# A Mamba-2 scan in the second layer of a two-layer kernel: squares summed ahead of the product with ones, and B held twice per chunk

## The chip, the core and the metric

The kernel runs on one core of a Trainium2 chip. Five engines run their own instruction streams and meet at semaphores: TensorE (PE; its weight loads are listed as PEld), VectorE (DVE), ScalarE (ACT), GpSimd (POOL) and SyncE (SP), which mostly issues DMAs. The metric is the device time in microseconds of one execution.

## What is computed

Four sequences of 512 tokens with 256 features pass through two layers. Each layer adds to the tokens the output of a state-space scan and that of a mixture of experts (a shared expert and 16 routed ones). The change lies in the scan of the second layer, a Mamba-2 block with 64 heads of 8 columns and a state of 128:

```python
proj = hidden_states @ in_proj_w.T
gate = proj[..., :D_IN]                       # D_IN = 512
xBC = proj[..., D_IN:D_IN + CONV_DIM]         # x (512), B (128), C (128)
...
conv = conv_b + sum((conv_w[:, i] * xp[:, i:i + l, :] for i in range(K)))   # K = 4
xBC = jax.nn.silu(conv)
...
Y_diag = jnp.einsum('bcthn,bcshn,bhcts,bcshp->bcthp', Ch, Bh, Lmat, x)
states = jnp.einsum('bcshn,bhcs,bcshp->bchpn', Bh, decay_states, x)
...
Y_off = jnp.einsum('bcthn,bchpn,bhct->bcthp', Ch, prev, jnp.exp(dA_cum))
...
y = y + D[None, None, :, None] * x
hg = y * jax.nn.silu(gate)
var = jnp.mean(hg * hg, axis=-1, keepdims=True)
y = hg * jax.lax.rsqrt(var + EPS) * norm_w
return y @ out_proj_w.T
```

## The kernel before

The second layer's scan (`scan1_tensor`, `scan1_scalar`, `scan1_vector`, `scan1_sync`) goes through the four sequences (b) one after the other. Features lie on the partitions, in groups of 128: four groups (G1 = 4) of x and of the gate, one of B (`xB`), one of C (`xC`). All of it is fp32 but for the decay matrices.

**Projections.** For each sequence ten products of 128x512 (NPROJ = 10; L1819). The first six are B, C and the four groups of x: ScalarE copies one out of its bank into `xpad` (L1914) and `cv` (L1915), VectorE adds three taps of the convolution (L2035), ScalarE takes tanh (L1888), VectorE finishes silu (`silu_of`, L1978) into `xB`, `xC` or `xb`. The silu of projection n-1 stands ahead of the convolution of projection n on VectorE. The last four are the gate (L1926, L2046). LATE = 3: the last output tile of the sequence before is made behind the fourth projection (n = 3).

**Chunk steps.** The 512 tokens are cut into 8 chunks (CH) of 64 (Q). In step s TensorE first makes bank `gb`: the products of B and C (L1831) in columns 0:64 and B transposed (L1833) in columns 64:192, both written twice, to partitions 0:64 and 64:128, since the two halves of the heads lie there; then x transposed (L1840), the new state of the chunk before (L1846), for each of four groups the exponents (L1809, L1811), the products with the masked matrix (L1860) of the chunk before, and at the end of the step the product of C with the state S (L1877, 64 rows wide). VectorE multiplies x with its weights (L2071), forms the masked matrices (`products`, L1985), and carries S on (L2083, L2088). Every second step closes a tile of 128 tokens: y is added up (L2059, L1869), `gated` (L1993) and `gate` (L2001) make `hg`, ScalarE squares it into `sq` (128 x 4 groups x 128 tokens, L1893), and from step 4 on `output` makes the out-projection of a tile (L1796, four products of 256 columns) and the sum of its squares over all 512 features: four products of `sq` with two columns of ones (L1798), accumulated. ScalarE copies both into `ob` (L1898). Tile 3 of a sequence is made among the next one's projections, and that of the last sequence at the very end, where `mean_square` and `add_scan1` follow.

**Order.** Everything is written by hand; a "tick" counter spreads the routed experts' work (three ticks for a tile of 128 rows, 48 tiles) over projections and groups: `expert_tensor` (L1374, L1380, L1386, L1393), `expert_scalar` (L1402 to L1417), `expert_vector` (L1425 and L1427, which makes `hid`, for which TensorE waits at L1380). It ends with the tenth projection of the last sequence. Banks 0 and 1 are a ring (`PIECES`, `make`, `take`, `taken`) for projections, `gb`, exponents and outputs. SyncE loads the decay rows `crow` of a chunk when S of the chunk before is ready (L1743), and the experts' weights (L1437, L1438).

## Time and profile before

| | us |
|---|---|
| median of 3 runs | 1323.91 (1321.68 to 1327.96) |
| profiled execution | 1332.39, its span 1330.7 |
| PE / DVE / ACT / POOL busy | 1078.8 / 897.7 / 492.1 / 451.5 |
| mean granted clock of TensorE | 0.898 |

The profile is of one execution; its durations hold for that one. The second layer's scan begins at 781 us and fills the rest of the span. A row of the timeline has the start, the duration, engine and line, what is written and read, and in brackets how long the engine had been idle and who released it. A matmul's duration reaches to the end of its passage through the array, so that neighbours overlap: what a product costs is the distance between starts. The chain of work that ended last has the same columns, but there the durations are those stretches that follow one another without overlap. An fp32 product leaves two records (xN counts records).

### The profile page before, as it was taken

The page shows a single profiled execution, that of the slowest core. Times are in us where ns is not written, and L with a number is a line of the kernel's source. Part 1 is how long each engine was busy: PE and PEld are TensorE (multiplying, and loading weights), DVE is VectorE, ACT ScalarE, POOL GpSimd, SP SyncE. Part 2 cuts the span into 40 slices and gives each one's busy share as a digit, 9 for nine tenths or more (in the row PEclk, how much of TensorE's full clock was granted, in tenths as well). Part 3 has the DMA queues.
Part 4 walks back from the last instruction along what each step waited for, and adds up shares of the span by engine and source line. Part 5 has one row for each costly group of instructions (what it writes and reads, how often), then busy time and mean ns, then how long its engine had stood idle before and what let it go on. Part 6 is the DMA issues. An engine that isn't in the chain of part 4 may idle for free.

```text
span 1330.7 us, 19215 instructions
## 1 busy us (share of the span) xinstructions
PE 1078.8 (81%) x6464; PEld 643.8 (48%) x6464; DVE 897.7 (67%) x1480; ACT 492.1 (37%) x1110; POOL 451.5 (34%) x334
## 2 busy tenths in 40 slices
PE   2989895877878778874767758999799979998795
PEld 2545453444444444443634434565455645555354
DVE  3287576789998889897355646565566565565685
ACT  2111032445544445541220134344444454344432
POOL 1000000588888888761100152233132323231000
PEclk9799898799998889986787888899899979899898
DMA  9900071488888878889520123444254424442111
GB/s 373 311 4 0 7 189 63 76 153 153 149 151 144 149 135 150 153 133 228 99 64 1 24 81 87 101 97 99 55 132 87 110 60 103 91 96 55 25 54 63
DMA packets 116997, 143.30 MB, mean 108 GB/s; under 512 B 35830, under 2 KB 103142, under 8 KB 116710
## 3 DMA queue, kind: packets, MB, share of 16 engines
q0 software_dynamic: 34464, 77.92, 32.4%
q1 hardware_dynamic: 82438, 64.14, 17.4%
q8 instruction: 55, 0.90, 0.3%
q14 instruction: 40, 0.33, 0.1%
HBM read 72.80 MB, written 39.46 MB: 84 GB/s over the span
## 4 chain that ended last, share of the span: by engine, by line
PE 49%; DVE 24%; DMA 9%; issue 6%; ACT 5%; POOL 4%; SPq 3%; ACTq 0%; DVEq 0%; POOLq 0%
PE bank L666 6%; PE bank L1386 4%; PE bank L678 4%; PE bank L1819 4%; PE bank L1393 4%; PE bank L979 3%; PE bank L1860 3%; DVE xnT L1112 3%; DMA sum<-yo,to_i 3%; DVE areaB L1112 2%; DVE cv L2035 2%; PE bank L1796 2%; PE bank L1809 2%; PE bank L1811 2%; DMA wr<-in_gate 2%
## 5 line engine op out<-in xcount | busy, mean ns | idle before, releaser
L1459 POOL DMA_INDIRECT sum<-yo,to_i x48 | 76.5, 1593 | 327.6 <-ACT yo L1413 317.5
L1139 POOL DMA_INDIRECT xg<-xn_d,token_i x80 | 97.3, 1217 | 252.6 <-DVE to_i L441 157.9
L1132 POOL DMA_INDIRECT sum<-yo,to_i x80 | 157.9, 1974 | 44.8 <-issue 33.4
L979 PE MATMUL bank<-areaA,xgT 128*128 x320 | 131.7, 540 | 26.2 <-ACT xgT L1036 16.7
L996 PE MATMUL bank<-areaA,hidT 88*128 x320 | 95.7, 424 | 41.6 <-ACT hidT L1046 32.8
L1985 DVE TENSOR_TENSOR areaD<-areaD,gb 128x512 f32<-128x512 f32 x128 | 87.7, 689 | 35.6 <-ACT areaD L1947 24.7
L1112 DVE TENSOR_TENSOR_SCAN xnT<-areaB,xnT 128x1024 f32<-128x1024 f32 x44 | 100.9, 2292 | 3.5
L1947 ACT ACTIVATE areaD<-bank 128x512 f32<-128x512 f32 x128 | 76.1, 596 | 66.5 <-PE bank L1811 61.5
L979 PEld LDWEIGHTS bank<-areaA,xgT 128*128 128x128 f32 x320 | 61.9, 213 | 72.6 <-issue 57.7
L1819 PE MATMUL bank<-xnT,w_in 128*128 128x512 f32 x160 | 88.1, 681 | 10.0 <-POOLq L1482 10.0
L996 PEld LDWEIGHTS bank<-areaA,hidT 88*128 88x128 f32 x320 | 57.7, 200 | 76.2 <-issue 71.1
L666 PE MATMUL bank<-xnT,areaB 128*128 128x512 f32 x192 | 88.4, 608 | 0.8 <-DVE y L696 0.8
L1028 ACT ACTIVATE areaB<-delta,a_neg 128x1022 f32<-128x1022 f32 x64 | 72.8, 1138 | 24.2 <-DVE y L1092 17.9
L2035 DVE SCALAR_TENSOR_TENSOR cv<-xpad,conv_w,cv 128x512 f32<-128x512 f32 x72 | 54.0, 750 | 25.8 <-ACT cv L1915 24.1
L1393 PE MATMUL bank<-wst,xgT 128*128 128x352 f32 x192 | 67.7, 476 | 0.0
L687 ACT ACTIVATE areaB<-bank 128x512 f32<-128x512 f32 x24 | 14.3, 597 | 135.9 <-PE bank L666 135.9
L1386 PE MATMUL bank<-wst,hidT 88*128 88x256 f32 x192 | 61.0, 446 | 1.8 <-ACT hidT L1407 1.2
L1860 PEld LDWEIGHTS bank<-areaD,xq 128*32 128x32 f32 x2048 | 35.1, 111 | 55.2 <-issue 43.0
L1041 ACT ACTIVATE act_t<-bank 128x176 f32<-128x176 f32 x80 | 25.2, 315 | 95.9 <-PE bank L979 91.6
L949 PE MATMUL bank<-parts,pick 96*128 96x512 bf16 x128 | 41.3, 406 | 23.0 <-DVE areaB L1116 10.7
L666 PEld LDWEIGHTS bank<-xnT,areaB 128*128 128x128 f32 x192 | 36.1, 194 | 48.5 <-issue 45.3
L678 PE MATMUL bank<-areaB,y 128*128 128x256 f32 x192 | 48.6, 414 | 13.3 <-DVE x L708 11.2
(329 smaller groups left out, 2271.7 us busy)
## 6 DMA issues: line engine op xcount, KB each, us to landing
y<-xnT POOLq DMA_DIRECT2D x22, 1024.0 KB
wst<-gu_f SPq DMA_DIRECT2D x96, 176.0 KB
y<-areaB POOLq DMA_DIRECT2D x10, 1024.0 KB
wst<-down_f SPq DMA_DIRECT2D x48, 176.0 KB
gu_f<-in_gu POOLq DMA_DIRECT2D x1, 5632.0 KB, 19.0
areaA<-in_gu SPq DMA_DIRECT2D x2, 2816.0 KB
sum<-yo SPq DMA_DIRECT2D x2, 2176.0 KB, 17.9
down_f<-in_down POOLq DMA_DIRECT2D x1, 2816.0 KB, 24.8
```

The source lines that it names most:

```text
L666: last = nc.tensor.matmul(bank[:, b, :], w[:, k, f * P:(f + 1) * P], xnT[:, k, c * 512:(c + 1) * 512], start=(k == 0), stop=(k == KD - 1))
L678: last = nc.tensor.matmul(bank[:, 4 + n % 2, 0:D], shT[:, (c * F + f) % shT.shape[1], j * P:(j + 1) * P], sd[:, f, :], start=(f == 0), sto ...
L979: last = nc.tensor.matmul(bank[:, GB + q % 2, 0:2 * FI], xgT[:, q % 2, k, :], wgu0_of(e, k), start=(k == 0), stop=(k == KD - 1))
L996: last = nc.tensor.matmul(bank[:, HY, 0:D], hidT[:, q % 2, h, :], wd0_of(e, h), start=(h == 0), stop=(h == 1))
L1112: nc.vector.tensor_tensor_scan(h, dA[:, u % 2, :], h, 0.0, ALU.mult, ALU.add).then_inc(da_free, 1)
L1132: nc.gpsimd.indirect_dma_start(sum0_d[q % 2], bass.IndirectOffsetOnAxis(ap=to_i[:, q:q + 1], axis=0), yo[:, q % 5, :], None, compute_op=AL ...
L1139: nc.gpsimd.indirect_dma_start(xg[:, q % 5, :], None, xn_d[0], bass.IndirectOffsetOnAxis(ap=token_i[:, q:q + 1], axis=0)).then_inc(s.gathe ...
L1386: last = nc.tensor.matmul(bank[:, eb, 0:D], hidT[:, (q - 1) % 2, h, :], wd_of(q - 1, h), start=(h == 0), stop=(h == 1))
L1393: last = nc.tensor.matmul(bank[:, eb, 0:2 * FI], xgT[:, q % 2, k, :], wgu_of(q, k), start=(k == 0), stop=(k == KD - 1))
L1819: last = nc.tensor.matmul(o, w_in[:, k, col:col + P], xnT[:, k, b * L:(b + 1) * L], start=(k == 0), stop=(k == KD - 1))
L1985: nc.vector.tensor_tensor(mm[:, g, :].rearrange("p (j t) -> p j t", t=Q), ex[:, g % 2, :].rearrange("p (j t) -> p j t", t=Q), gb[:, step % ...
L2035: last = nc.vector.scalar_tensor_tensor(cv[:, n % 2, :], xpad[:, n % 2, i:i + L], conv_w[:, j, i:i + 1], cv[:, n % 2, :], ALU.mult, ALU.add)
```

## The change

`sum_squares` on VectorE adds the four groups of `sq` into `sq_sum` (128x128) with one reduce, and TensorE waits for it (`sq_summed`) ahead of the whole output; one product with ones remains. `xB` now holds each chunk's 64 columns twice, written by two silu instructions, and each product for `gb` has all 128 columns as its weight and writes both halves at once. The reduces for tiles 0 to 2 stand at the third group of steps 4, 6 and 8, behind `products` and ahead of the addition to S, those for tile 3 behind the third projection's convolution of the next sequence, and the last one behind the last `gate`.

```diff
--- before.py
+++ after.py
@@ -1260,9 +1260,10 @@
         cv = sb("cv", [P, 2, L], F32, c1)
         tb = sb("tb", [P, 2, L], F32, c1)
         xb = sb("xb", [P, G1, L], F32, c1)
-        xB = sb("xB", [P, L], F32, c1)
+        xB = sb("xB", [P, CH, 2, Q], F32, c1)
         xC = sb("xC", [P, L], F32, c1)
         sq = sb("sq", [P, G1, P], F32, c1)
+        sq_sum = sb("sq_sum", [P, P], F32, c1)
         ob = sb("ob", [P, PAIRS, D + 2], F32, c1)
         dw = sb("dw", [P, 2, CH, NB, HP], F32, c1)
         ecn = sb("ecn", [P, PAIRS, NB, HP, 2], F32, c1)
@@ -1293,6 +1294,7 @@
             sem(n) for n in ("xt_full", "xt_used", "st_full", "s_ready", "yo_full", "m_ready", "m_used"))
         y_tok, yt_full, y_read, hg_ready, sq_ready, ssq_in, ssq_out, x_done = (
             sem(n) for n in ("y_tok", "yt_full", "y_read", "hg_ready", "sq_ready", "ssq_in", "ssq_out", "x_done"))
+        sq_summed = sem("sq_summed")
         crow_in = [sem(f"crow_in{k}") for k in range(2)]
         cpc_in = [sem(f"cpc_in{k}") for k in range(2)]
         dec_in = [sem(f"dec_in{k}") for k in range(2)]
@@ -1791,12 +1793,10 @@
             def output(b, t):
 
                 o, full = make(pe, b, "out", t)
-                pe.wait_ge(sq_ready, b * PAIRS + t + 1)
+                pe.wait_ge(sq_summed, b * PAIRS + t + 1)
                 for g in range(G1):
                     nc.tensor.matmul(o[:, 0:D], hg[:, g, t * P:(t + 1) * P], w_out[:, g, :], start=(g == 0), stop=(g == G1 - 1))
-                for g in range(G1):
-                    last = nc.tensor.matmul(o[:, D:D + 2], sq[:, g, :], ones[:, 0:2], start=(g == 0), stop=(g == G1 - 1))
-                last.then_inc(full, 1)
+                nc.tensor.matmul(o[:, D:D + 2], sq_sum[:, :], ones[:, 0:2], start=True, stop=True).then_inc(full, 1)
 
             def segment(b, step, g):
 
@@ -1827,11 +1827,9 @@
                     at = slice(step * Q, (step + 1) * Q)
                     if step < CH:
                         o, full = make(pe, b, "gb", step)
-                        for r in (0, Q):
-                            nc.tensor.matmul(o[r:r + Q, 0:Q], xB[:, at], xC[:, at], start=True, stop=True)
-                        for r in (0, Q):
-                            last = nc.tensor.matmul(o[r:r + Q, Q:Q + P], xB[:, at], ident[:, :], start=True, stop=True)
-                        last.then_inc(full, 1)
+                        both_b = xB[:, step, :, :].rearrange("p r t -> p (r t)")
+                        nc.tensor.matmul(o[:, 0:Q], both_b, xC[:, at], start=True, stop=True)
+                        nc.tensor.matmul(o[:, Q:Q + P], both_b, ident[:, :], start=True, stop=True).then_inc(full, 1)
 
                         if b * CH + step:
                             pe.wait_ge(xt_used, b * CH + step)
@@ -1974,8 +1972,14 @@
             def silu_of(b, n):
                 v.wait_ge(conv_tanh, b * 6 + n + 1)
                 j = CONV_ORDER[n]
-                to = (xb[:, j, :] if j < G1 else (xB, xC)[j - G1][:, :])
-                nc.vector.scalar_tensor_tensor(to, tb[:, n % 2, :], 1.0, cv[:, n % 2, :], ALU.add, ALU.mult).then_inc(conv_out, 1)
+                if j == G1:
+                    by_chunk = [z[:, n % 2, :].rearrange("p (k t) -> p k t", t=Q) for z in (tb, cv)]
+                    for r in range(2):
+                        last = nc.vector.scalar_tensor_tensor(xB[:, :, r, :], by_chunk[0], 1.0, by_chunk[1], ALU.add, ALU.mult)
+                else:
+                    to = xb[:, j, :] if j < G1 else xC[:, :]
+                    last = nc.vector.scalar_tensor_tensor(to, tb[:, n % 2, :], 1.0, cv[:, n % 2, :], ALU.add, ALU.mult)
+                last.then_inc(conv_out, 1)
 
             def products(b, step, g):
 
@@ -1999,6 +2003,14 @@
                 at = slice(t * P, (t + 1) * P)
                 v.wait_ge(y_read, b * PAIRS + t + 1)
                 nc.vector.scalar_tensor_tensor(hg[:, :, at], hg[:, :, at], 0.5, gz[:, :, at], ALU.mult, ALU.mult).then_inc(hg_ready, 1)
+
+            def sum_squares(b, t):
+
+                v.wait_ge(sq_ready, b * PAIRS + t + 1)
+                if b or t:
+                    n = b * PAIRS + t - 1
+                    taken(v, n // PAIRS, "out", n % PAIRS)
+                nc.vector.tensor_reduce(sq_sum[:, :], sq[:, :, :].rearrange("p g t -> p t g"), X, ALU.add).then_inc(sq_summed, 1)
 
             def mean_square(b):
 
@@ -2044,6 +2056,8 @@
                         o, free = take(v, b, "proj", n)
                         v.wait_ge(gate_th, b * G1 + g + 1)
                         nc.vector.scalar_tensor_tensor(gz[:, g, :], tb[:, g % 2, :], 1.0, o, ALU.add, ALU.mult).then_inc(free, 1)
+                    if b and n == LATE - 1:
+                        sum_squares(b - 1, PAIRS - 1)
                     if b and n == LATE + 1:
                         mean_square(b - 1)
                     if b and n == LATE + 3:
@@ -2076,6 +2090,8 @@
                         expert_vector(v, step_tick(b, step, g))
                         if step < CH:
                             products(b, step, g)
+                        if g == 2 and step % 2 == 0 and step > 2:
+                            sum_squares(b, (step - 4) // 2)
                         if g == 1 and 1 < step < CH:
                             v.wait_ge(yo_full, b * (CH - 1) + old)
                             state_of(v, b, old)
@@ -2096,6 +2112,7 @@
                         add_experts(SUMS.index(step))
                 gated(b, PAIRS - 1)
                 gate(b, PAIRS - 1)
+            sum_squares(NB - 1, PAIRS - 1)
             mean_square(NB - 1)
             add_scan1(NB - 1)
             add_experts(NB - 1)
```

The lines of the changed kernel have other numbers: L1798 is then the out-projection (before L1796), L1799 the product with ones (L1798), L1832 B transposed (L1833), L1838 x transposed (L1840), L1844 the state (L1846), L1875 C with S (L1877), L1867 y added up (L1869), L1989 `products` (L1985), L2104 the addition to S (L2088), L2013 the reduce.

TensorE at the turn from step 4 to 5 of the first sequence, before: `ys` added up, the output, C with S, then the chunk's own products.

```order
L1869 MATMUL bank<-ident,ys 128x128 x4
L1796 MATMUL bank<-w_out,areaD 128x256 x4
L1798 MATMUL bank<-ones,sq 128x2 x4
L1877 MATMUL bank<-S,xC 64x512
L1831 MATMUL bank<-xC,xB 64x64 x2
L1833 MATMUL bank<-ident,xB 64x128 x2
L1840 MATMUL bank<-ident,xb 64x64 x8
L1846 MATMUL bank<-xd,gb 128x512
```

The same place in the changed kernel:

```order
L1867 MATMUL bank<-ident,ys 128x128 x4
L1798 MATMUL bank<-w_out,areaD 128x256 x4
L1799 MATMUL bank<-ones,sq_sum 128x2
L1875 MATMUL bank<-S,xC 64x512
L1831 MATMUL bank<-xC,xB 128x64
L1832 MATMUL bank<-ident,xB 128x128
L1838 MATMUL bank<-ident,xb 64x64 x8
L1844 MATMUL bank<-xd,gb 128x512
```

The order is the same; three products with ones are gone, and two full-width products (128 rows) stand where four of 64 rows stood, between others of 64 rows.

VectorE in a step 6, from the decay of S to the gated tile, before (`act_t` and `hid` are the expert's):

```order
L2083 TENSOR_TENSOR S<-S,dec 128x512 [waits s_ready,yo_full]
L1425 SCALAR_TENSOR_TENSOR act_t<-act_t,bank 128x176 [waits tanh_ready1]
L1427 SCALAR_TENSOR_TENSOR hid<-act_t,bank 128x176 [waits vec]
L1985 TENSOR_TENSOR areaD<-areaD,gb 128x512 [waits m_used,ring_free0]
L2088 TENSOR_TENSOR S<-S,bank 128x512 [waits vec,st_full]
L1985 TENSOR_TENSOR areaD<-areaD,gb 128x512 [waits m_used,ring_free1]
L1993 SCALAR_TENSOR_TENSOR areaD<-xb,d_head,bank 128x128 [waits yt_full]
```

and in the changed kernel:

```order
L2099 TENSOR_TENSOR S<-S,dec 128x512 [waits s_ready,yo_full]
L1427 SCALAR_TENSOR_TENSOR act_t<-act_t,bank 128x176 [waits tanh_ready1]
L1429 SCALAR_TENSOR_TENSOR hid<-act_t,bank 128x176 [waits vec]
L1989 TENSOR_TENSOR areaD<-areaD,gb 128x512 [waits m_used,ring_free0]
L2013 TENSOR_REDUCE sq_sum<-sq 128x128 [waits ring_free1,sq_ready]
L2104 TENSOR_TENSOR S<-S,bank 128x512 [waits vec,st_full]
L1989 TENSOR_TENSOR areaD<-areaD,gb 128x512 [waits m_used,ring_free1]
L1997 SCALAR_TENSOR_TENSOR areaD<-xb,d_head,bank 128x128 [waits yt_full]
```

The reduce stands ahead of the addition to S and of the last group's masked matrix. The other new row of VectorE is the second silu of B, directly behind the first.

## Rows read from the trace of the kernel before

**Rows 1.** The page's part 4: shares of the chain that ended last, by engine.

```profile
PE 49%; DVE 24%; DMA 9%; issue 6%; ACT 5%; POOL 4%; SPq 3%; ACTq 0%; DVEq 0%; POOLq 0%
```

**Rows 2.** Busy time by stretch: length, PE, PEld, DVE, ACT, POOL, clock, DMA.

```profile
966.00:1069.00 103.00, 97.57 (x1007) 59.41 (x1005) 62.36 (x127) 46.79 (x114) 33.99 (x26) 1.00 0.49 110
...
1245.00:1321.00 76.00, 67.14 (x900) 39.38 (x898) 56.42 (x107) 27.15 (x52) 1.55 (x1) 0.99 0.18 54
```

**Rows 3.** Groups by line, 660 to 1331 us: busy us, mean ns, idle before.

```profile
L1798 PE MATMUL bank<-ones,sq 128*128 128x2 f32 x128 | 15.9, 247 | 0.0
```

**Rows 4.** Timeline of PE, a chunk's own products, sequence 1.

```profile
989.45 0.33 PE L1831 MATMUL bank<-xC,xB 128*64 128x64 f32 x2
...
989.92 0.59 PE L1877 MATMUL bank<-S,xC 128*64 128x512 f32 x1
...
991.24 0.70 PE L1846 MATMUL bank<-xd,gb 128*128 128x512 f32 x1
```

**Rows 5.** Timeline of PE at three turns between widths.

```profile
982.34 0.43 PE L1860 MATMUL bank<-areaD,xq 128*32 128x64 f32 x16
982.70 0.42 PE L1380 MATMUL bank<-ident,hid 128*88 128x128 f32 x2
982.96 0.38 PE L1809 MATMUL bank<-crow,sel_c 70*128 70x512 bf16 x1
...
1013.75 0.95 PE L1798 MATMUL bank<-ones,sq 128*128 128x2 f32 x8
1014.63 0.64 PE L1877 MATMUL bank<-S,xC 128*64 128x512 f32 x1
...
1058.05 0.95 PE L1798 MATMUL bank<-ones,sq 128*128 128x2 f32 x8
1058.86 0.68 PE L1819 MATMUL bank<-xnT,w_in 128*128 128x512 f32 x1
```

**Rows 6.** Groups of DVE by line: a strided reduce, the silu of B.

```profile
L349 DVE TENSOR_REDUCE area<-area 128x256 f32<-128x512 f32 x1 | 0.7, 698 | 0.0
...
L1978 DVE SCALAR_TENSOR_TENSOR xB<-tb,cv 128x512 f32<-128x512 f32 x4 | 2.8, 692 | 3.4 <-ACT tb L1888 3.4
```

**Rows 7.** The chain that ended last: start, us on the chain, what.

```profile
789.61 0.69 DVE xB L1978
...
927.32 0.69 DVE xB L1978
...
937.35 1.50 PE bank L1798 x8
938.85 3.62 PE bank L1819 x4
...
1001.27 3.28 DMA crow<-cp_d
...
1056.49 1.73 PE bank L1796 x8
...
1059.00 1.82 PE bank L1819 x4
...
1066.44 0.69 DVE xB L1978
```

**Rows 8.** Timeline of the projections of sequences 1 and 3.

```profile
934.55 0.42 PE L1380 MATMUL bank<-ident,hid 128*88 128x128 f32 x2 [3.95 <-DVE hid L1427]
...
1219.58 0.69 DVE L1978 SCALAR_TENSOR_TENSOR xC<-tb,cv 128x512 f32<-128x512 f32 x1 [1.94 <-ACT tb L1888]
```

**Rows 9.** Timeline of step 6, last sequence: DVE's third group, PE's output.

```profile
1298.40 0.68 DVE L1985 TENSOR_TENSOR areaD<-areaD,gb 128x512 f32<-128x512 f32 x1
...
1299.39 1.89 PE L1796 MATMUL bank<-w_out,areaD 128*128 128x256 f32 x8
```

**Rows 10.** Timeline of the last tile: squares and output.

```profile
1316.71 0.62 ACT L1893 ACTIVATE sq<-areaD 128x512 f32<-128x512 f32 x1
...
1317.48 1.97 PE L1796 MATMUL bank<-w_out,areaD 128*128 128x256 f32 x8 [1.08 <-ACT sq L1893]
```

## The prediction

> **What bounds the kernel now.** First the shares of the chain that ended last [rows 1]: TensorE holds 49% of it, VectorE 24%. The change touches only the second layer's scan, so the stage is read next [rows 2]. In the chunk steps of sequence 1 (966 to 1069) TensorE is busy 97.6 of 103 us and VectorE 62.4; in those of the last sequence (1245 to 1321), which has no expert work between, 67.1 and 56.4 of 76. So in the steps a product saved on TensorE shortens the run and VectorE has room, if the instruction doesn't stand ahead of something that TensorE waits for. Between the steps, in the projections, it is otherwise: there the chain runs VectorE, ScalarE, VectorE (silu, convolution, tanh) and TensorE stands idle 3.95 us before it gets its next operand [rows 7, 8]. What matters is then who is ahead of whom on VectorE. Each fp32 product leaves two records in the trace.
>
> **Squares on TensorE (gain).** The four products with ones leave 8 records, 128 over 16 tiles [rows 3]. Eight take from 1058.05 to 1058.86, 0.81 us, 0.10 each [rows 5], though only two columns stream: the weight is what is paid for. One product keeps two records, 0.20 us, so 0.61 us go. All 16 sit between work of TensorE that waits for them, so 16 x 0.61 = -9.8 us. One of them runs at the lower clock (1.50 us for eight [rows 7]) and could give 1.1; if the clock comes back at the same moment anyway, it gives 0.6, which I take.
>
> **B twice (four products become two).** Here the count misleads. The four products are 64 columns wide and go in pairs to the lower and the upper half of the array's output; the trace shows the halves running side by side: two L1831 records start at 989.45, before the second record of L1877 at 989.92 and on the half that L1877 leaves free [rows 4]. The clean measure is the stretch from the second L1877 record to L1846: 989.92 to 991.24, 1.32 us [rows 4], and the same pair of rows gives 1.32 or 1.33 in all 24 chunks that have an L1877 ahead. 512 columns of fp32 take 0.43 (eight records of 256 take 1.73 [rows 7], 0.216 each), 64 take 0.05, 128 take 0.11. The stretch is then, for one half of the array: rest of L1877 0.43, two of 64 columns 0.11, two of 128 columns 0.21, eight of L1840 0.43: 1.18, and 0.14 are left for the change from half-width back to full-width products.
> Other rows show that a change of width costs something. Eight L1798 records followed by a full-width product take 0.81; followed by the half-width L1877 they take 0.88 (1013.75 to 1014.63) [rows 5]: 0.07 for going narrow. Sixteen records of the 32-wide L1860 are four deep, 4 x 0.053 = 0.21, and take 0.36 until L1380 [rows 5]: 0.15 for going wide. The two full-width records of L1380 take 0.26 rather than 0.21 [rows 5], so 0.05 for a first weight that nothing hides.
> The changed kernel puts two full-width products between L1877 and L1840, which are both half-width: two changes of width more per chunk. The stretch becomes 0.43 + 0.15 (wide) + 0.20 (two records of 64 columns, bound by their weight as L1798 is) + 0.26 (two of 128) + 0.07 (narrow) + 0.43 + 0.15 = 1.69 or so, against 1.32: **+0.38 us**, a loss. Ends: +0.09 if the two changes cost nothing (0.41 for four full records, 0.32 before), +0.50 if going narrow costs as much as going wide and the weight is exposed again.
> The Trainium skill, TensorEngine Tiling (Array Packing), Key Properties, speaks against this change: changing the tiling mode drains TensorE, while different tiles load and multiply in parallel. By its rule both added changes are paid, by a count of products the pair would have gained; the two intervals above agree with it, and it gives no price.
> In 4 of these 24 chunks the chain goes through the load of crow instead (3.28 us at 1001 [rows 7]) and the loss is hidden: 20 x 0.38 = +7.6. The 8 chunks at steps 0 and 1 have no L1877 ahead and come from full width: there 0.38 less one change each way of 0.15 and 0.07, +0.15, so 8 x 0.15 = +1.2. Together **+8.8** (ends +1.8 and +12).
>
> **The second write of B.** One more silu of 128x512, 0.69 us [rows 6], in each of four projections, right behind the first and ahead of the next convolution. The first write at 927.32 is itself in the chain [rows 7], and so are those of sequences 0 and 2; in sequence 3 VectorE then idles 1.94 us for ScalarE [rows 8] and hides it. 3 x 0.69 = +2.1 (ends 0 and 2.8: other work may take its place, or sequence 3 may not hide it).
>
> **The reduces.** 16 of 128x512 to 128x128. The row nearest, a reduce of 512 elements read with a stride, takes 0.70 us [rows 6]. Twelve stand at the third group of steps 4, 6 and 8, ahead of the addition to S; in sequences 0 to 2 the steps are longer by expert work and VectorE is busy for 62.4 of 103 us [rows 2]; at each of those nine places the reduce ends before TensorE has come to the output, so they cost nothing; if that cover were gone, up to 0.7 each. S itself is only needed after the output block (1.73 + 0.81 us of TensorE). In the last sequence the cover is short: products end at 1299.08, the reduce would end near 1299.8, and the output could have started at 1299.39 [rows 9]: TensorE waits 0.45, in steps 4 and 6 alike, +0.9. Those of the fourth tile stand at the third projection behind its convolution: in sequence 1 expert_vector comes right behind and TensorE waits for its hid [rows 8], +0.7; in the two others VectorE waits for tanh there and nothing is due. At the very end the order is squares, reduce, output with nothing beside it: squares start at 1316.71, the output at 1317.48 [rows 10]; the reduce and its signal add 0.75. Sum +2.35 (ends +0.7 and +5).
> The Trainium skill, VectorE: DVE Perf Modes, calls tensor_reduce the slowest op of this engine, to be restructured away on a hot path; here 0.70 against 0.69 for the silu of the same size [rows 6], so the sum doesn't change.
>
> **Sum.** -9.8 + 8.8 + 2.1 + 2.35 = **+3.5 us**. The profiled execution took 1332.39, which would become 1335.9; it was 8.5 above the median of the three timed runs. On that median: 1323.91 + 3.5 = 1327.4. With the widths at their low end -3.5, at their high end +6.7.
>
> **Rivals.**
> A, changes of width are nearly free (+0.09 per chunk): -9.8 + 1.8 + 4.5 = -3.5, 1320.4. For it: part of the 0.15 may be the weight load, which 128-wide products pay anyway. Against it: 0.81 and 0.88 for the same eight records.
> B, fewer products is simply less work, as the change says: if the four ran one after the other they would cost 0.64, the two 0.41, so 28 x -0.23 = -6.4, and the reduces hide: -9.8 - 6.4 + 4.5 = -11.7, 1312.2. Against it stands the 1.32 us stretch, too short for products in a row.
> C, slower: the clock. TensorE stands idle 3.95 us before 934.55 and then runs at the lower of its two levels for some microseconds: a projection takes 3.62 where it otherwise takes 1.82 [rows 7, 8]. The added silu and reduce stretch this idle to 5.3 in sequence 1 and lengthen it in two others. If each of the four projections then has one more piece at 1.2 GHz, 4 x 1.8 = +7.2 on top of 3.5: 1334.6. It decides from the point where the longer idle time makes the slow stretch last one projection longer; for it, the slow stretch is longest where the idle time is; against it, the clock already falls there today.
>
> **How the numbers follow.** My forecast (1327.4, its own range 1320 to 1332) 0.60, A 0.14, B 0.08, C 0.18. The bound of what can be told is 0.5%, 6.6 us. Faster by more: B, and a little of A: 0.10. Slower by more: C, and the upper tail of the forecast, where widths cost +0.50 and reduces are less covered (+6.7 and more): 0.23. Within: 0.67. The range leaves out B and the far part of C: 1317.5 to 1334.
>
> **What would show it.** Right: from the second record of the state product to the next S product 1.6 to 1.8 us instead of 1.32; ones products 0.2 per tile; outputs of the last sequence waiting some 0.4 us for the reduce, the very last 0.7; silu of B twice in the chain of three projections. Wrong: a stretch of 1.4 or less (A, B); a lower granted clock in the projections than now, or low stretches in other places (C); reduces much over 0.7 us, or a load of crow that is now late behind a later S.

## The result, and the profile after

Over 17 runs each, taken together, the changed kernel has a median of 1335.99 us and the kernel before 1324.67; the ratio is 1.0064 [1.0041, 1.0087]. On the 1323.91 us of the first table that is +8.5 us (+5.4 to +11.5), 1332.4. The sign was forecast, the size (+3.5) was not; 1332.4 lies in the range, the bare median 2 us above it.

The profiled execution took 1339.03 us, its span is 1337.2, its clock 0.890. The first line of the page's part 1, then groups by line from 660 us to the end (busy us, mean ns, idle before and who ended it):

```profile
PE 1089.7 (81%) x6240; PEld 642.3 (48%) x6240; DVE 915.7 (68%) x1500; ACT 493.1 (37%) x1110; POOL 454.5 (34%) x334
```

```profile
L1798 PE MATMUL bank<-w_out,areaD 128*128 128x256 f32 x128 | 35.0, 422 | 4.8 <-DVE sq_sum L2013 4.8
...
L2013 DVE TENSOR_REDUCE sq_sum<-sq 128x128 f32<-128x512 f32 x16 | 16.6, 1035 | 1.1 <-ACT sq L1891 1.1
L1832 PE MATMUL bank<-ident,xB 128*128 128x128 f32 x64 | 14.7, 312 | 0.0
L1831 PE MATMUL bank<-xC,xB 128*128 128x64 f32 x64 | 13.7, 297 | 0.6 <-ACT areaD L1945 0.6
```

Two things stand out. A reduce takes 1.03 us, not the 0.70 of [rows 6], and TensorE waits 4.8 us for it ahead of the out-projection, where the forecast had 0.9 and 0.75. VectorE is busy 18.0 us longer than before, 16.6 of them in the reduces.

The timeline of TensorE in sequence 1, the place of [rows 4] (start, us, line; brackets give idle time and releaser):

```profile
988.27 1.07 PE L1875 MATMUL bank<-S,xC 128*64 128x512 f32 x2
...
989.28 0.43 PE L1831 MATMUL bank<-xC,xB 128*128 128x64 f32 x2
...
989.55 0.44 PE L1832 MATMUL bank<-ident,xB 128*128 128x128 f32 x2
...
989.92 0.69 PE L1838 MATMUL bank<-ident,xb 128*64 128x64 f32 x16
...
990.53 1.12 PE L1844 MATMUL bank<-xd,gb 128*128 128x512 f32 x2
```

From the first record of C with S to the state product it takes 2.26 us; before, 1.80 (1.32 from the second record, now 1.78). It is 2.26 in 23 of the 24 chunks, +0.46 each; the remaining one, at 1258.87, takes 4.11 with a granted clock of 0.50. The full-width L1831 starts only 1.01 us behind the first L1875 record, near the end of the second; none of the new products runs beside another.

The last tile, the place of [rows 10], all engines:

```profile
1321.34 0.62 ACT L1891 ACTIVATE sq<-areaD 128x512 f32<-128x512 f32 x1
1321.99 1.02 DVE L2013 TENSOR_REDUCE sq_sum<-sq 128x128 f32<-128x512 f32 x1 [1.05 <-ACT sq L1891]
...
1323.15 3.40 PE L1798 MATMUL bank<-w_out,areaD 128*128 128x256 f32 x8 [2.14 <-DVE sq_sum L2013]
...
1326.34 0.43 PE L1799 MATMUL bank<-ones,sq_sum 128*128 128x2 f32 x2
```

TensorE now stands idle for 2.14 us, where it was 1.08, and the eight records take 3.40 us instead of 1.97: they run at 1.2 GHz. Busy time by stretch, with the granted clock behind POOL's column, says so for these 3.2 us:

```profile
1323.10:1326.30 3.20, 3.15 (x8) 2.57 (x9) 0.00 (x0) 0.00 (x0) 0.00 (x0) 0.57 0.00 0
```

The projections of sequence 1, pieces of the chain that ended last (durations without overlap), the place of [rows 7, 8]:

```profile
925.59 1.29 DVE xB L1978 x2
...
932.66 1.02 DVE sq_sum L2013
933.68 0.26 DVE act_t L1427
...
933.96 0.35 DVE hid L1429
...
934.36 0.66 PE bank L1382 x2
935.01 3.18 PE bank L1798 x8
```

Both silu writes and the reduce lie on it, ahead of `hid`. The two writes lie on the chain in sequences 0 and 2 as well (788.21 and 1063.40), each time 1.29 us where one write took 0.69. TensorE's idle time there is 5.48 us, against 3.95 [rows 8]; the prediction had 5.3. TensorE's timeline has this row, and the output of the fourth tile of sequence 2, which comes in the projections of sequence 3:

```profile
934.36 0.66 PE L1382 MATMUL bank<-ident,hid 128*88 128x128 f32 x2 [5.48 <-DVE hid L1429]
...
1217.31 3.36 PE L1798 MATMUL bank<-w_out,areaD 128*128 128x256 f32 x8 [1.89 <-DVE sq_sum L2013]
```

This wait of 1.89 us was not in the sum at all. In sequence 1 the longer idle time of this execution did not make the low stretch longer: from `hid`'s product to the end of the next projection it takes 5.77 us (934.36 to 940.13), before 7.92 (934.55 to 942.47), since the clock fell earlier and came back earlier.

One caution for all that follows. Where the clock is low differs from execution to execution. The profiled one of the changed kernel ran the first steps of its last sequence at 1.2 GHz until about 1265.5 (a state product takes 2.01 on the chain there, 1.05 before); in others that stretch is at 2.4. And the second layer's scan, the only part that differs, begins anywhere from 775 to 790 us in the fourteen profiled executions. So a whole profile's length is no decomposition of a median, and sizes below come from the ratios, places from the traces.

### The profile page after: what moved, and what is told of

Same layout as the page of the kernel before. It is cut to its first block, busy times and chain, and to the rows that moved or that the text cites. A ratio compares the mean times of both kernels' runs of the same rounds, so it can differ in the third digit from the quotient of the medians.

```text
span 1337.2 us, 18802 instructions
## 1 busy us (share of the span) xinstructions
PE 1089.7 (81%) x6240; PEld 642.3 (48%) x6240; DVE 915.7 (68%) x1500; ACT 493.1 (37%) x1110; POOL 454.5 (34%) x334
## 4 chain that ended last, share of the span: by engine, by line
PE 34%; DVE 9%; DMA 5%; ACT 3%; issue 2%; POOL 2%; SPq 1%; ACTq 0%; POOLq 0%; DVEq 0%
PE bank L1395 4%; PE bank L1388 4%; PE bank L1819 3%; PE bank L1858 3%; DMA sum<-yo,to_i 3%; PE bank L1798 2%; PE bank L1809 2%; DVE cv L2047 2%; PE bank L1844 2%; PE bank L666 2%; PE bank L1811 2%; PE bank L1875 2%; PE bank L1838 1%; PE bank L1382 1%; DMA crow<-cp_d 1%
## 5 line engine op out<-in xcount | busy, mean ns | idle before, releaser
L1132 POOL DMA_INDIRECT sum<-yo,to_i x80 | 160.1, 2002 | 44.4 <-issue 37.3
L1989 DVE TENSOR_TENSOR areaD<-areaD,gb 128x512 f32<-128x512 f32 x128 | 87.9, 689 | 28.3 <-ACT areaD L1945 27.3
L949 PE MATMUL bank<-parts,pick 96*128 96x512 bf16 x128 | 41.4, 407 | 23.1 <-DVE areaB L1116 10.9
```

Source lines behind the costliest of these rows:

```text
L1132: nc.gpsimd.indirect_dma_start(sum0_d[q % 2], bass.IndirectOffsetOnAxis(ap=to_i[:, q:q + 1], axis=0), yo[:, q % 5, :], None, compute_op=AL ...
L1989: nc.vector.tensor_tensor(mm[:, g, :].rearrange("p (j t) -> p j t", t=Q), ex[:, g % 2, :].rearrange("p (j t) -> p j t", t=Q), gb[:, step % ...
```

## The experiments

Each ratio is against the kernel before in the same series (median 1326.86 us for the first four below, 1327.29 for the next four, 1326.05 for the last four).

**The two parts alone.** First the squares, with `xB` as it was: only `sq_sum`, the reduce and one product with ones.

```diff
-                pe.wait_ge(sq_ready, b * PAIRS + t + 1)
+                pe.wait_ge(sq_summed, b * PAIRS + t + 1)
...
-                for g in range(G1):
-                    last = nc.tensor.matmul(o[:, D:D + 2], sq[:, g, :], ones[:, 0:2], start=(g == 0), stop=(g == G1 - 1))
-                last.then_inc(full, 1)
+                nc.tensor.matmul(o[:, D:D + 2], sq_sum[:, :], ones[:, 0:2], start=True, stop=True).then_inc(full, 1)
```

> The squares part alone: one reduce on VectorE and one product with ones, B held once and its four narrow products as before. Theory 1 (the products of B pay for changes of width, the squares part gains): ones products -9.8 us; reduces, measured 1.03 us each in the changed kernel, on the path at one projection (+1.0), twice in the last sequence (+0.8 each) and at the very end (+1.1): together about -6 us against before. Theory 2 (the loss comes from the reduces, which push VectorE's work back everywhere): +3 us or more against before. Theory 3 (the loss is the clock, which falls more often whatever is changed): this kernel too shows more time at the low level in its last sequence than before, and is not faster.

Measured 1324.50 us, 0.9982 [0.9948, 1.0016]: -2.4 us (-6.9 to +2.1). The loss of +3 that theory 2 expected is out; the gain of 6 that theory 1 expected is inside the interval. The last tile, all engines:

```profile
1307.22 0.62 ACT L1893 ACTIVATE sq<-areaD 128x512 f32<-128x512 f32 x1
1307.87 1.02 DVE L2009 TENSOR_REDUCE sq_sum<-sq 128x128 f32<-128x512 f32 x1 [1.04 <-ACT sq L1893]
...
1309.04 3.64 PE L1798 MATMUL bank<-w_out,areaD 128*128 128x256 f32 x8 [2.14 <-DVE sq_sum L2009]
...
1312.51 0.28 PE L1799 MATMUL bank<-ones,sq_sum 128*128 128x2 f32 x2
```

The same wait and the same fall of the clock as in the changed kernel, without B's part. The outputs in steps 4 and 6 of the last sequence wait 0.63 and 0.62 us here.

Then B twice alone, with the four products of `sq` as they were.

```diff
-        xB = sb("xB", [P, L], F32, c1)
+        xB = sb("xB", [P, CH, 2, Q], F32, c1)
...
+                        both_b = xB[:, step, :, :].rearrange("p r t -> p (r t)")
+                        nc.tensor.matmul(o[:, 0:Q], both_b, xC[:, at], start=True, stop=True)
+                        nc.tensor.matmul(o[:, Q:Q + P], both_b, ident[:, :], start=True, stop=True).then_inc(full, 1)
```

> The B part alone: xB written twice, two full-width products per chunk; squares and ones products as before. Theory 1: the stretch from the first record of C with S to the state's product is 2.26 us instead of 1.80 in 24 chunks; 20 of them on the path give +9.2, the 8 others some +1.5, the second silu +2.1: about +12.8 us against before. Theory 2 (reduces): this kernel is no slower than before by more than the silu, +2 us. Theory 3 (clock): slower by low stretches in the last sequence, with the count of chunks explaining less than half of it.

Measured 1336.15, 1.0080 [1.0044, 1.0116]: +10.6 us (+5.8 to +15.4). The two parts add up to +8.2, the whole is +8.5. TensorE's timeline:

```profile
994.25 1.07 PE L1877 MATMUL bank<-S,xC 128*64 128x512 f32 x2
...
995.25 0.43 PE L1833 MATMUL bank<-xC,xB 128*128 128x64 f32 x2
...
995.52 0.44 PE L1834 MATMUL bank<-ident,xB 128*128 128x128 f32 x2
...
995.89 0.69 PE L1840 MATMUL bank<-ident,xb 128*64 128x64 f32 x16
...
996.51 1.12 PE L1846 MATMUL bank<-xd,gb 128*128 128x512 f32 x2
```

2.26 us from L1877 to L1846 here too.

**The second silu apart from the wide products.** `xB` is written twice, and the four products of 64 columns are kept.

```diff
-                            nc.tensor.matmul(o[r:r + Q, 0:Q], xB[:, at], xC[:, at], start=True, stop=True)
+                            nc.tensor.matmul(o[r:r + Q, 0:Q], xB[:, step, r // Q, :], xC[:, at], start=True, stop=True)
                         (and the same for the two products with ident)
```

> B written twice, but the four narrow products per chunk as before (they read one copy each for the two halves); squares as before. What is left is four silu instructions of 0.69 us. Theory 1: +2.1 us against before (three of the four are on the path). If the longer idle time of TensorE in the projections costs clock as the third rival of the prediction said: +5 us or more, with more time at the low level than before.

Measured 1329.84, 1.0033 [0.9997, 1.0069]: +4.4 us by the ratio (-0.4 to +9.2), +3.0 between the medians. That leaves room for both of the expectations, the +2.1 of the silu alone and the +5 with the clock; the mean clock over the runs is 0.899 against 0.902 before. The stretch is 1.80 us again in 23 chunks, and 3.31 in one at a granted clock of 0.52. The full-width products alone are then 10.6 - 4.4 = +6.2, by differences with several us of uncertainty. The traces agree in size where the clock allows a comparison: the chunk steps of sequence 1 ran at a granted clock of 1.00 in all fourteen traces, and from the first state product to the first product of the next projections they take 87.64 us before (971.22 to 1058.86), 87.99 with the second silu alone (967.65 to 1055.64) and 89.22 with the wide products too (964.05 to 1053.27), one execution each.

**Waiting late for the sum.** The squares' part, with the out-projection waiting for `hg` alone, and only the product with ones for the sum.

```diff
-                pe.wait_ge(sq_summed, b * PAIRS + t + 1)
+                pe.wait_ge(hg_ready, b * PAIRS + t + 1)
                 for g in range(G1):
                     nc.tensor.matmul(o[:, 0:D], hg[:, g, t * P:(t + 1) * P], w_out[:, g, :], start=(g == 0), stop=(g == G1 - 1))
+                pe.wait_ge(sq_summed, b * PAIRS + t + 1)
```

> As the squares part alone, but TensorE waits for hg ahead of the out-projection and for the sum only ahead of the product with ones. Theory 1: the waits for the reduce in the last sequence go (1.6 us) and the last tile's out-projection starts without squares and reduce ahead of it (about 1 us there): -8.5 us against before, 2 to 3 us better than the squares part alone. Theory 2 (reduces hold VectorE's own queue, not TensorE's output): no difference between the two.

Measured 1318.77, 0.9943 [0.9909, 0.9977]: -7.6 us, so 5.2 better than with the early wait, where 2 to 3 was expected. That this is close to the prediction's -7.45 for the squares (-9.8 + 2.35) is chance: most of the waits in the 2.35 are gone here. The last tile:

```profile
1311.47 1.97 PE L1798 MATMUL bank<-w_out,areaD 128*128 128x256 f32 x8 [0.19 <-DVE areaD L2002]
...
1312.26 1.04 DVE L2010 TENSOR_REDUCE sq_sum<-sq 128x128 f32<-128x512 f32 x1 [0.93 <-ACT sq L1894]
...
1313.35 0.38 PE L1800 MATMUL bank<-ones,sq_sum 128*128 128x2 f32 x2
```

TensorE waits 0.19 us and keeps 2.4 GHz; squares and reduce lie beside the out-projection. From the start of the last `gate` to ScalarE's copy of the last bank it takes 3.14 us here (1310.63 to 1313.77), 6.69 with the early wait (1306.14 to 1312.83) and 5.19 before (1315.08 to 1320.27). So 3.55 of the 5.2 us lie in this one place.

**Squares laid out for the reduce.** As the last, and ScalarE writes the four groups next to each other.

```diff
-        sq = sb("sq", [P, G1, P], F32, c1)
+        sq = sb("sq", [P, P, G1], F32, c1)
...
-                nc.scalar.activation(sq[:, :, :], hg[:, :, t * P:(t + 1) * P], ACT.Square).then_inc(sq_ready, 1)
+                nc.scalar.activation(sq[:, :, :].rearrange("p t g -> p g t"), hg[:, :, t * P:(t + 1) * P], ACT.Square).then_inc(sq_ready, 1)
...
-                nc.vector.tensor_reduce(sq_sum[:, :], sq[:, :, :].rearrange("p g t -> p t g"), X, ALU.add).then_inc(sq_summed, 1)
+                nc.vector.tensor_reduce(sq_sum[:, :], sq[:, :, :], X, ALU.add).then_inc(sq_summed, 1)
```

> As the kernel that waits late for the sum (squares part alone), but ScalarE writes the squares with the four groups side by side, so that the reduce reads without a stride. If the stride of 512 bytes is what makes the reduce 1.03 us instead of the 0.70 of the row in the trace before, it now takes 0.70 us; two reduces are on the path (sequence 1's projection, the last tile), so -0.7 us against the late-waiting kernel, which is too little to tell by the time; the duration tells. If the reduce costs 1.03 us for its 128 results whatever the stride, its duration stays, and ScalarE's square may get longer than 0.63 us.

Measured 1316.00, 0.9929 [0.9899, 0.9959]: -9.4 us, not to be told from the -7.6. The groups by line:

```profile
L1894 ACT ACTIVATE sq<-areaD 128x512 f32<-128x512 f32 x16 | 18.1, 1132 | 3.6 <-DVE areaD L2002 3.6
...
L2010 DVE TENSOR_REDUCE sq_sum<-sq 128x128 f32<-128x512 f32 x16 | 10.9, 678 | 1.4 <-ACT sq L1894 1.4
```

The reduce falls from 1.03 to 0.68 us, and the square rises from 0.63 to 1.13.

**B's part with its products behind x transposed**, where the array stays in halves from C with S to x.

```diff
                         (the products of xb with ident, last.then_inc(xt_full, 1))
+                        o, full = make(pe, b, "gb", step)
+                        both_b = xB[:, step, :, :].rearrange("p r t -> p (r t)")
+                        nc.tensor.matmul(o[:, 0:Q], both_b, xC[:, at], start=True, stop=True)
+                        nc.tensor.matmul(o[:, Q:Q + P], both_b, ident[:, :], start=True, stop=True).then_inc(full, 1)
```

> The B part alone (second silu, two full-width products), but the two products stand behind the eight narrow transposes of x and ahead of the full-width state product, so that no change of width is added. Theory 1 (changes of width cost): the stretch from the first record of C with S to the state's product falls from 2.26 to about 1.95 us, and the kernel is 4 to 8 us faster than the B part with the products in front, some +4 to +7 us against before, of which the silu is +4.4. Rival (what is lost is only that two narrow products ran side by side): the stretch stays above 2.15 and the kernel is as slow as the B part alone (+10.6 us).

Measured 1328.72, 1.0006 [0.9974, 1.0038]: +0.8, 9.8 us better than with the same products in front, and better than the 4 to 8 that was expected from the widths. TensorE's timeline:

```profile
986.06 0.64 PE L1876 MATMUL bank<-S,xC 128*64 128x512 f32 x1
986.07 0.33 PE L1835 MATMUL bank<-ident,xb 128*64 128x64 f32 x2
986.54 0.59 PE L1876 MATMUL bank<-S,xC 128*64 128x512 f32 x1
986.97 0.63 PE L1835 MATMUL bank<-ident,xb 128*64 128x64 f32 x14
987.53 0.43 PE L1840 MATMUL bank<-xC,xB 128*128 128x64 f32 x2
...
987.80 0.44 PE L1841 MATMUL bank<-ident,xB 128*128 128x128 f32 x2
988.07 1.02 PE L1845 MATMUL bank<-xd,gb 128*128 128x512 f32 x2
```

Two records of x transposed lie beside the first of L1876, and the stretch is 2.01 us in all 24 chunks. That is 0.25 less than 2.26, in 32 chunks at most 8 us. But the place was moved too, which the ninth kernel below takes apart.

**Both orders mended in the changed kernel** (the late wait, and the products behind x).

> The changed kernel with both orders mended: B's full-width products behind the transposes of x, and the wait for the sum only ahead of the product with ones. Theory 1: the parts add up: squares with the late wait -7.6 us, B behind x +4 to +7: between -4 and 0 us against before, some 10 us faster than the changed kernel. If the parts don't add (one hides the other): as the changed kernel, +8.5.

Measured 1312.02, 0.9901 [0.9864, 0.9938]: -13.1 us, where the two parts by themselves give -7.6 + 0.8 = -6.8, and between -4 and 0 was expected. With two of its instructions elsewhere the changed kernel is a gain of 1%; the tenth kernel below is as fast without B's part.

**The reduces behind what others wait for**, on the kernel with the squares laid out and the late wait: behind the addition to S, and in the projections behind the expert's `hid`.

```diff
-                        if g == 2 and step % 2 == 0 and step > 2:
-                            sum_squares(b, (step - 4) // 2)
                         (the addition to S)
+                        if g == 2 and step % 2 == 0 and step > 2:
+                            sum_squares(b, (step - 4) // 2)
```

> The late-waiting squares part with contiguous squares, and the reduces moved behind the work that others wait for: behind the addition to S in the steps, behind the expert's hid in the projections. Theory 1: only the reduce ahead of hid in sequence 1 was on the path (1 us or 0.7), so -0.7 us against the kernel with contiguous squares. Theory 2 (the reduce ahead of S and of the masks costs in many steps): 3 us faster or more than that kernel.

Measured 1313.89, 0.9914 [0.9883, 0.9945]: -11.4, 2 us better than without, inside the intervals.

**The narrow products behind x, and nothing else changed.**

```diff
                         (the products of xb with ident, last.then_inc(xt_full, 1))
+                        o, full = make(pe, b, "gb", step)
+                        for r in (0, Q):
+                            nc.tensor.matmul(o[r:r + Q, 0:Q], xB[:, at], xC[:, at], start=True, stop=True)
+                        for r in (0, Q):
+                            last = nc.tensor.matmul(o[r:r + Q, Q:Q + P], xB[:, at], ident[:, :], start=True, stop=True)
+                        last.then_inc(full, 1)
```

> The kernel before with one thing moved: its four narrow products of B stand behind the eight narrow transposes of x. Everything is the same work at the same widths. It tells whether the gain of the B part behind x came from the widths or from the place. Theory 1 (widths): TensorE's stretch stays 1.80 us and the time is that of before, within 2 us. Rival (place: VectorE gets x earlier, and starts its chain earlier): 3 us faster or more.

Measured 1322.67, 0.9937 [0.9898, 0.9977]: -8.4 us, where my theory expected at most 2 to either side. This ratio is over the seven shortest of twelve runs, one of them a very short one of 1305.07. Over all runs but one of 1747.67 the median is 1322.08 and the ratio about 0.9956 (0.992 to 0.999 by my working): -6 us, or -4 between the medians. The stretch is still 1.80 us in all 24 chunks, so the gain isn't there. VectorE gets x earlier: its waits for x transposed (us in total, times, longest), first of the kernel before and of this one, then of B twice alone and of the same with its products behind x:

```profile
DVE xq L2071 <- PE bank L1840: 32.6, 17, 3.2
```

```profile
DVE xq L2070 <- PE bank L1833: 25.8, 13, 2.9
```

```profile
DVE xq L2085 <- PE bank L1840: 44.2, 26, 3.7
```

```profile
DVE xq L2084 <- PE bank L1835: 26.0, 13, 2.9
```

The move takes 6.8 us off this wait for the narrow products and 18.2 for the wide ones, and both then wait alike. The steps of each sequence, taken as above, had the same mean clock in the traces of the kernel before and of this one, and there the move gives 0.6, 1.5 and 2.0 us in sequences 0, 1 and 2 and nothing in the last: -4.0 us. So of the 9.8 us that the move gave to the wide products some 4 to 8 are the place, and the width is left with the rest.

**The two good moves without the change to B** (late wait, narrow products behind x), and **the same with the reduces behind** the addition to S and `hid`.

> The squares part with the late wait, and the narrow products of B behind x: the kernel with both orders mended, but without the second silu and without full-width products. Theory 1 (widths): as the squares part with the late wait, -7.6 us against before. Rival (place): -11 us or more, as fast as or faster than the kernel with both orders mended (-13.1), because it is without the second silu (+4.4 when alone).

> As the one before, with the reduces behind the addition to S and behind the expert's hid. If the reduce ahead of them is what is left of the reduces' cost, 1 to 2 us faster than the one before; this is the candidate for the fastest of the study.

Measured 1312.22, 0.9891 [0.9849, 0.9932], and 1307.46, 0.9861 [0.9824, 0.9898]: -14.5 and -18.4 us. Here the parts nearly add up: -7.6 and -4 to -8. The first is as fast as the changed kernel with both orders mended (-13.1), without anything of B's part. The second has the lowest median of this study and holds no second silu and no full-width product for `gb`. Its difference to the first, 4 us, is again within the intervals, as the 2 us above were.

**The changed kernel with the late wait alone.**

> The changed kernel with the late wait for the sum alone; B's full-width products stay ahead of the transposes of x, with their two changes of width. Theory 1 (the parts add): the changed kernel's +8.5 less the 5.2 us that the late wait gave in the squares part, so +3 us against before; the kernel with both orders mended is then some 10 us faster, which is what the B part gained from its place alone (+10.6 to +0.8). If the parts don't add: below 0.

Measured 1322.96, 0.9967 [0.9934, 1.0000]: -4.4 us by the ratio, 12.9 better than the changed kernel (the two intervals together leave some 5 us to either side). Moving one wait made of a slower kernel one that isn't. But the same move gave 5.2 us with B's part absent. The traces show 3.4 us of it at the last tile and 0.41 in two steps; and in sequence 3, without the wait of 1.89 and the low clock behind it, the tenth projection comes 37.3 us behind the first instead of 40.5, 3.2 us less: 7.4 together. The rest is about what the intervals leave. The mean clock over the runs is 0.903 with the late wait and 0.898 without, so more time at 1.2 GHz in the changed kernel may be part of it; where that time lies over the runs isn't shown.

## Where the prediction was right and where it was wrong

**The squares** were mis-sized: forecast -9.8 + 2.35 = -7.45, measured -2.4. The interval of that measurement (-6.9 to +2.1) leaves the forecast just outside. The saving of three products fits the -7.6 that was measured without the early wait. Three steps of the +2.35 failed, all on the wait:
- The reduce was priced at 0.70 by the nearest row; it takes 1.03.
- At the very end the term was the reduce's 0.75. The idle time did grow by 1.06 us (1.08 to 2.14), and then the clock fell: 3.40 and 3.64 us instead of 1.97 in the two kernels with the early wait, 1.96 or 1.97 in every other of this study. From `gate` to ScalarE's copy +1.4 (6.56 against 5.19), where -0.61 + 0.75 = +0.14 was forecast.
- For the fourth tile in sequences 2 and 3 "nothing is due" was wrong in one: 1.89 us at 1217.31, again with a low clock behind it (3.36).

The 0.45 us each in steps 4 and 6 of the last sequence came as 0.41 and 0.41. I argued for the wait's place as given and never asked what TensorE needs the sum for: the out-projection doesn't read it.

**B twice** was right in its mechanism. Forecast 8.8 + 2.1 = 10.9, measured 10.6, a match closer than the interval of some 5 us to either side, and in part luck: its two terms were off in opposite ways. The stretch grew by 0.46 us, not 0.38, near the upper end of 0.50; the wide products apart are +6.2 (forecast 8.8), the silu +3 to +4.4 (2.1), each uncertain by several us. That a count of products is no count of time (rival B, 1312.2) is shown: two in place of four are longer in every chunk that the stretch measures. (The chain before goes through the load of `crow` five times, at 836.84, 862.94, 1001.27, 1134.42 and 1173.34, not four as the prediction counted; by its own terms that is 0.4 us.) Rival A (+0.09 per chunk) fell by the same stretch. The Trainium skill, TensorEngine Tiling (Array Packing), Key Properties, has a change of mode drain the array; the trace agrees in so far as two changes in a chunk, together with the loss of products side by side, cost 0.46 us, and it doesn't tell the two apart. What I overlooked is the place: these products also stood ahead of x, for which VectorE waits, and moving them alone is worth some 4 to 8 us in the kernel before.

**Rival C, the clock,** was half right. The longer waits at the last tile (+1.4 us) and in a projection are each followed by a low stretch; but not one more piece of 1.8 us in each of four projections: in the profiled executions the projections of sequences 1 and 3 have one low stretch of 3.4 us more than before, those of sequence 2 one less, those of sequence 0 as many. The mean clock over the runs is 0.898 for the changed kernel, the lowest here, 0.900 to 0.902 for the kernel before, and 0.903 with B twice alone, the slowest part, so the clock doesn't order the kernels. But the difference isn't nothing. An estimate from these means: 0.003 of a span of 1334 us is 2 x 0.003 x 1334 = 8 us more at 1.2 GHz, worth up to 4, and the two places behind the waits, 3.4 us each, are most of it. It is a term in the squares' wait, as far as the traces show, and the parts measured alone show that it isn't what makes the change a loss.

**The total**: +3.5 forecast, +8.5 [+5.4, +11.5] measured. Of the 5 us missing, all are the squares' part by the ratios (-2.4 for -7.45), each of which is uncertain by some 5 us; B's came out as forecast. The chance of slower by over 0.5% was 0.23, and that is what the ratio says, if barely. The low chance came from treating the waits ahead of the output as 0.45 and 0.75 us with nothing behind them. Two of the prediction's own signs of being wrong came: reduces well over 0.7 us, and low stretches in other places.

**Still open**: how much of B's +6.2 is width and how much the wait for x (behind x, the wide products with the second silu are 5 to 9 us worse than the narrow ones by the sixth and ninth kernels, but only 1.4 us worse by the seventh and tenth). The traces side with the smaller: in the steps of sequence 1 the wide products behind x take 0.1 us more than the narrow ones (86.26 against 86.15), and with the late wait 0.3 (84.52 against 84.25), in the last sequence 0.4 (59.33 against 58.95), all at a granted clock of 1.00. And open is how much of the 12.9 us of the late wait in the changed kernel is the clock.

## What to carry to other kernels

The runs bear out three rules for a kernel like this one. Put a wait directly ahead of the first instruction that reads the data: a partial result that only one small product needs must not hold back the large ones that could cover its making. Before you merge small products into a larger one, look whether they run side by side in the parts of the array; if they do, a smaller count can be more time, above all between products of another width. And test an instruction's place by itself, with no other edit: here two moves gave more than the change.

## What the runs showed of the hardware

- A reduce of 128x512 to 128x128, four elements to a result: 1.03 us read with a stride of 128 elements, 0.68 read contiguously. The strided reduce of the same input with 256 results of two took 0.70 [rows 6], so the size of the input alone doesn't give the price. It differs from the 1.03 both in the stride (16 elements) and in the elements to a result; which of the two counts isn't shown.
- ScalarE's square of 128x512 takes 0.63 us written in order and 1.13 us written with a stride of four elements; the time that the reduce saves is paid there.
- With two changes of width between half-width products, and nothing side by side, 0.46 us more in a chunk than four half-width products; with one change moved to where one was needed anyway, 0.21 more (2.01 against 1.80).
- The chunk steps of sequence 0 at a lower clock: 94.13 us in the changed kernel, with 6.8 us at 1.2 GHz, and 89.98 with the late wait and none at 1.2. In sequence 1, at 1.00 in both, they take 85.97 and 86.12.
- TensorE idle for 1.08 us ahead of the last output, behind busy steps: the next eight records at 2.4 GHz (1.97 us). Idle for 2.14 us: at 1.2 GHz (3.40 and 3.64), in both kernels where this occurs, one execution each; that the idle time is what made the clock fall is likely, not shown.
